# Attention scores of a chunk: three split fp32r passes in four row groups, or one fp32 pass straight from the projections

## The reference, cut to what matters

```
q = silu(to_heads(q)); k = silu(to_heads(k)); v = to_heads(v)
qkv_none_diag = einsum('bhmd,bhde->bhme', qi * q_decay, kv)
qk       = einsum('bhmd,bhsd->bhms', qi, ki) * diag_decay
qkv_diag = einsum('bhms,bhse->bhme', qk, vi)
kv_new   = block_decay * kv + einsum('bhsd,bhse->bhde', ki * k_decay, vi)
```

## Time and profile before

| | |
|---|---|
| time, 3 runs | median 572.98 us, 571.99 to 573.39 |
| profiled execution | its own time 572.29 us, span of its trace 570.6 us |
| TensorE busy | 514.4 us, 90% of the span |
| VectorE, ScalarE, GpSimd busy | 328.6, 262.3, 247.3 us |
| mean granted TensorE clock | 0.961 of full speed |

### The profile page before, as it was taken

The page is one execution under the profiler, slowest core; times in us unless marked ns, Lnnn a source line. Parts: engine busy times, 40 slices in busy tenths (PEclk is TensorE's granted clock), DMA queues, the critical chain, the costliest instruction groups (busy, mean ns, idle before and its releaser), DMA issues.

```text
span 570.6 us, 11414 instructions
## 1 busy us (share of the span) xinstructions
PE 514.4 (90%) x4523; PEld 472.3 (83%) x4523; DVE 328.6 (58%) x613; ACT 262.3 (46%) x472; POOL 247.3 (43%) x207
## 2 busy tenths in 40 slices
PE   2979999999999999999999479889989997399994
PEld 2969899998999989999898469778967876399983
DVE  5988655754387787644547855778764643012331
ACT  7822232222276668232433337656676744253340
POOL 2062454333231333343386847243433333068973
PEclk9979999999999999999999787999998998799998
DMA  8733133211311001022224315543348331424532
GB/s 258 278 96 119 47 112 112 93 57 38 112 40 36 24 20 39 20 66 69 109 93 148 116 56 174 192 166 130 118 160 277 100 138 40 147 76 152 176 115 37
DMA packets 32884, 62.11 MB, mean 109 GB/s; under 512 B 3440, under 2 KB 3456, under 8 KB 32704
## 3 DMA queue, kind: packets, MB, share of 16 engines
q1 hardware_dynamic: 32288, 60.08, 31.5%
q0 software_dynamic: 544, 1.31, 1.2%
HBM read 48.27 MB, written 13.12 MB: 108 GB/s over the span
## 4 chain that ended last, share of the span: by engine, by line
PE 58%; issue 17%; POOL 10%; DVE 8%; ACT 5%; DMA 1%; SPq 0%; DVEq 0%; POOLq 0%; ACTq 0%
PE bank L1264 19%; PE bank L1218 7%; PE bank L1219 7%; PE bank L1220 7%; PE bank L1255 6%; POOL wlo L1162 5%; PE bank L1286 3%; DVE rope L897 2%; PE bank L1332 2%; PE bank L1322 2%; PE bank L1294 2%; PE bank L1316 2%; PE bank L1234 1%; DMA UR<-uo_all 1%; DVE rope L895 1%
## 5 line engine op out<-in xcount | busy, mean ns | idle before, releaser
L1162 POOL TENSOR_TENSOR wlo<-raw,whi 128x512 fp32r<-128x512 f32 x96 | 129.9, 1386 | 122.4 <-ACT whi L521 122.4
L1218 PE MATMUL bank<-HTh,whi 128*128 128x256 f32 x224 | 66.3, 296 | 14.4 <-DVE XR L932 9.7
L1219 PE MATMUL bank<-HTl,whi 128*128 128x256 f32 x224 | 65.8, 294 | 0.0
L1220 PE MATMUL bank<-HTh,wlo 128*128 128x256 f32 x224 | 65.5, 292 | 0.0
L1143 POOL TENSOR_TENSOR state<-kv_new,state_dec 128x512 f32<-128x512 f32 x15 | 21.8, 1454 | 94.7 <-DVE kv_new L834 94.7
L823 DVE TENSOR_TENSOR A<-bank,DEC 128x512 f32<-128x512 f32 x64 | 39.7, 683 | 37.2 <-PE bank L1286 35.7
L1218 PEld LDWEIGHTS bank<-HTh,whi 128*128 128x128 f32 x224 | 45.5, 203 | 15.4 <-issue 15.1
L521 ACT ACTIVATE whi<-raw 128x2048 fp32r<-128x2048 f32 x24 | 45.8, 1910 | 16.5 <-DMA raw<-in_w_down 12.5
L1219 PEld LDWEIGHTS bank<-HTl,whi 128*128 128x128 f32 x224 | 45.5, 203 | 0.2
L1220 PEld LDWEIGHTS bank<-HTh,wlo 128*128 128x128 f32 x224 | 45.4, 203 | 0.0
L1264 PE MATMUL bank<-xTh,WKh 128*128 128x256 f32 x128 | 38.6, 302 | 2.1 <-DVE WKl L764 2.1
(11 more groups left out here) (281 smaller groups left out, 1539.4 us busy)
## 6 DMA issues: line engine op xcount, KB each, us to landing
X<-in_x SPq DMA_DIRECT2D x16, 256.0 KB, 2.9
xn_all<-XN SPq DMA_DIRECT2D x16, 256.0 KB, 2.0
uo_all<-uo SPq DMA_DIRECT2D x16, 256.0 KB, 2.6
raw<-in_wq SPq DMA_DIRECT2D x4, 1024.0 KB, 5.3
UR<-uo_all SPq DMA_DIRECT2D x16, 256.0 KB, 5.6
XR<-in_x SPq DMA_DIRECT2D x16, 256.0 KB, 4.7
raw<-in_wo SPq DMA_DIRECT2D x4, 1024.0 KB, 5.6
out<-XR SPq DMA_DIRECT2D x16, 256.0 KB, 2.9
```

The source lines that it names most:

```text
L1162: ins = Q.tensor_tensor(low[:, k, :], raw[b % 2][:, k, :], high[:, k, :].bitcast(f32), ALU.subtract)
L1218: T.matmul(dst, lh, rh, start=first, stop=False)
L1219: T.matmul(dst, lh, rl, start=False, stop=False)
L1220: return T.matmul(dst, ll, rh, start=False, stop=last)
```

## The change

`score` multiplies chunk N of KT and QT as they stand, as 16 fp32 matmuls (one for each head) instead of 48 fp32r ones. kh, kl, qh and ql, the four steps that write them and their semaphores are gone. `score` waits for the projections alone; the evacuation of new K and Q projections (`evacuate`) waits for the scores that read the old ones.

```diff
-        kh, kl, qh, ql = (at(n, 112 + 2 * i, [P, NK, P], f32r) for i, n in enumerate(("kh", "kl", "qh", "ql")))
...
                     if name == "K":
-                        act.wait_ge(q_w_lo if g else k_w_lo, NK), act.wait_ge(k_lo, used)
-                        act.wait_ge(kt_ps, used), act.wait_ge(k_hi, used)
+                        act.wait_ge(q_w_lo if g else k_w_lo, NK), act.wait_ge(s_ps, used), act.wait_ge(kt_ps, used)
                     if name == "Q":
-                        act.wait_ge(q_w_lo, NK), act.wait_ge(q_lo, used), act.wait_ge(q_dec, used)
-                        act.wait_ge(q_hi, used)
+                        act.wait_ge(q_w_lo, NK), act.wait_ge(s_ps, used), act.wait_ge(q_dec, used)
...
-            def k_high(N):
-                act.wait_ge(proj_sb, NPROJ * (N // CH) + 2)
-                act.wait_ge(s_ps, N), act.wait_ge(k_lo, N)
-                S.activation(kh[:], chunk(KT, N), ACT.Copy).then_inc(k_hi, 1)
-
-            def q_high(N):
-
-                act.wait_ge(proj_sb, NPROJ * (N // CH) + 4)
-                act.wait_ge(s_ps, N), act.wait_ge(q_lo, N)
-                S.activation(qh[:], chunk(QT, N), ACT.Copy).then_inc(q_hi, 1)
...
-            def q_low(N):
-                dve.wait_ge(q_hi, N + 1), dve.wait_ge(s_ps, N)
-                V.tensor_tensor(ql[:], chunk(QT, N), qh[:].bitcast(f32), ALU.subtract).then_inc(q_lo, 1)
...
-            def k_low(N):
-                pool.wait_ge(k_hi, N + 1)
-                Q.tensor_tensor(kl[:], chunk(KT, N), kh[:].bitcast(f32), ALU.subtract).then_inc(k_lo, 1)
...
             def score(N):
 
-                pe.wait_ge(k_hi, N + 1), pe.wait_ge(q_hi, N + 1)
-                pe.wait_ge(k_lo, N + 1), pe.wait_ge(q_lo, N + 1)
-                pe.wait_ge(masked, 4 * N)
+                pe.wait_ge(proj_sb, NPROJ * (N // CH) + 4), pe.wait_ge(masked, 4 * N)
...
                 for j in range(NK):
-                    for n, (k, q) in enumerate(((kh, qh), (kh, ql), (kl, qh))):
-                        for r in range(4):
-                            rows = slice(DH * r, DH * r + DH)
-                            ins = T.matmul(score_banks[r][:, j * P:(j + 1) * P], k[rows, j, :], q[rows, j, :],
-                                           start=n == 0, stop=n == 2)
+                    for r in range(4):
+                        rows = slice(DH * r, DH * r + DH)
+                        ins = T.matmul(score_banks[r][:, j * P:(j + 1) * P], chunk(KT, N)[rows, j, :],
+                                       chunk(QT, N)[rows, j, :], start=True, stop=True)
                 ins.then_inc(s_ps, 1)
```

More of the change, by code:

```diff
@@ L268, in build @@
         xt_ps, xt_hi, xt_lo, proj_ps, proj_sb = sems("xt_ps xt_hi xt_lo proj_ps proj_sb")
-        k_hi, q_hi, k_lo, q_lo, q_dec, kt_ps, k_dec = sems("k_hi q_hi k_lo q_lo q_dec kt_ps k_dec")
+        q_dec, kt_ps, k_dec = sems("q_dec kt_ps k_dec")
         s_ps, masked, inter_ps, kv_ps, kv_masked, pv_ps = sems("s_ps masked inter_ps kv_ps kv_masked pv_ps")
@@ L592, in _ @@
                 in_position(N, 0, tiles)
-                if N == -1:
-                    k_high(0)
-                    q_high(0)
                 if N >= 1:
                     mean_square(N - 1)
-                if 0 <= N < N_TILES - 1:
-                    k_high(N + 1)
-                    q_high(N + 1)
                 count_marks(ranked(N, 0))
@@ L970, in _ @@
                     key_decayed(N)
-                if -1 <= N < N_TILES - 1:
-                    q_low(N + 1)
                 in_position(N, 0)
@@ L1173, in _ @@
                     q_decayed(N)
-                if -1 <= N < N_TILES - 1:
-                    k_low(N + 1)
                 if N == HIDDEN:
```

## The result

The changed kernel takes **565.84 us** (median of 4 runs, 564.69 to 566.58), against 573.18 us for the kernel before (median of 4 runs, 571.99 to 576.35; three of them are those of the table of the time before). The medians are 7.3 us apart. The recorded ratio is 0.9853, 95% interval 0.9816 to 0.9889, so the change is faster by 6.4 to 10.5 us. The forecast was 564.5. The profiled execution took 566.07 us (span 564.3), 6.2 us less than the profiled one of before.

The account below looks back on a forecast made before the run. TensorE was taken to bound chunks 0 to 14, with a chain of waits in slot 14. Savings of 6.7 us on scores and 1.8 us in slot 14 sum to 8.5: 572.98 - 8.5 = 564.5 us, range 562 to 579.

Parts of the forecast that it names:

- The sets: Scores on TensorE: an fp32 set in row groups costs a weight load, 0.112 us; 8 sets a chunk instead of 12.
- The rival by the Trainium skill: Scores on TensorE: an fp32 matmul's two records hold each other up; 1.94 us a chunk, 578.2 us; chance 0.12.
- One matmul at a time: Scores on TensorE: fp32 matmuls in row groups don't run side by side; 3.73 us a chunk, 606.6 us; chance 0.07.
- the bound of 0.54 us a chunk: Scores on TensorE: upper bound of the saving, if a set costs only 0.10 us.
- the other 0.15 us is the entry and the exit: A chunk's scores on TensorE: 0.15 us besides the sets, kept unchanged, so 1.49 us becomes 1.04.
- 15 x 0.45: Chunks 0 to 14 on TensorE: each saves 0.45 us where TensorE never waits, 6.7 us together.
- Slot 14: Chain of 300 to 325 us: 1.1 us without ql, 0.6 to 0.7 from a faster rotation; together 1.8 us.
- the rotation gets shorter: VectorE in slot 14: the rotation, 1.77 us beside kl, loses 0.6 to 0.7 us without kl.
- The chain behind it: After slot 14: all moves by 1.8 us; TensorE's wait before unit 4 shrinks to about 0.5, block 3's stays about 6.2.
- Behind 325.57 I take the rest as rigid: After unit 5's start at 325.57 us: no instruction changes, so what follows is taken as rigid.

Follow-up runs that it names:

- e4: Kernel before with the third fp32r pass (kl by qh) of the scores left out, all four split steps kept; 568.15 us.
- e3: Changed kernel with the two loops of score exchanged, all four column tiles of one row group before the next group; 591.59 us.
- e7: Kernel before with the change for chunk 15 alone: its scores in fp32, its four splits dropped; 570.83 us against 572.34.
- e1: Kernel before with fp32 scores and the added waits in evacuate, but kh, qh, ql and kl still computed and unread; 565.14 us.
- e2: Changed kernel with one subtraction of ql's shape put back on VectorE, in slot 14 alone, without kl on GpSimd; 566.66 us.
- a0: The changed kernel run a second time, with no edit; 565.78 us.
- e5: Changed kernel with weight block 3 split earlier: high part ahead of chunk 14's square, low part ahead of chunk 14's state; 562.94 us.
- e9: The kernel of e1 run again on another chip, with no edit; 566.06 us.

## Why the prediction was right, and where not

**The sets: right, and the rival fell.** The forecast hung on one step, that an fp32 set in row groups costs a weight load, 0.112 us, as the fp32r sets do. It does from the second set on, in every chunk, and e4 shows that eight sets cost nearly the same in either type. The rival by the Trainium skill, "TensorE: Matmul & The Clock Gate", section "The mechanism", went by a list item there that lets a load overlap matmuls in flight only if the row group differs; it would have made 1.94 us a chunk and 578.2 us. The loads of one row group start every 0.112 us and so do its fp32 streams of 0.106; one after the other they would need 0.21. The trace disagrees with that item, and the measurement decides. The paragraph ahead of it in the same section has a second condition that the rival left out, a load into the background weight buffer, which is also pulled ahead; no run here shows that buffer. One matmul at a time (606.6 us) fell too. What it feared exists in another order: e3 pays 2.75 us a chunk.

One of the bounds was a misreading. The prediction took 0.81 / 8 = 0.10 us a record from the earlier trace rows. The first two of those records start 0.03 us apart, and from the second on they follow at 0.112 us, so the bound of 0.54 us a chunk had nothing under it.

**The chunk's saving: 0.38, not 0.45.** The step that failed is "the other 0.15 us is the entry and the exit", carried over unchanged. With fp32 the entry is 0.05 to 0.06 us longer (e4). Over 14 chunks the miss is 14 x 0.45 - 5.37 = 0.9 us.

**"15 x 0.45": one chunk too many.** Chunk 14's scores lie before the waits, but their saving went into one: TensorE could have come to unit 1 6.2 us earlier, but block 1's low part came only 5.77 earlier (295.40 to 289.63), and the wait for it grew from 0.29 to 0.69. The prediction counted waits from 312 us on and left out the first, 0.29 us long, which already made TensorE a follower at 300 us. Cost: its 0.45 us.

**Slot 14: right size, wrong shares.** The prediction gave 1.8 us, 1.1 for ql and 0.6 to 0.7 for a rotation that is no longer slowed by kl. Measured 1.68 in the change and 1.72 in e7. The shares came out the other way round, 0.6 for ql and 1.1 for kl (e1, e2, a0). The step that failed is that the rotation gets shorter: it stayed at 1.74, since qdec slows it now, as qdec slowed ql before (1.33 in e7, where it starts later beside qdec). What falls away is a whole turn of GpSimd's queue. Two rows could have told it: the rotation's end, 302.13 + 1.77 = 303.90, stands just behind kl's, 301.60 + 1.76 = 303.36.

**The chain behind it: right.** The wait before unit 4 was to shrink to about 0.5 us (0.62) and that for block 3 to stay at 6.2 (6.17). It also named what would be late next, the state of chunk 14 between the two blocks; e5 takes that away and gains 2.8 us.

**"Behind 325.57 I take the rest as rigid": right for the change by luck, wrong as a step.** Between 300 and 350 us the change has 17.1 us at the low clock, the same as before it, so the shift of 7.45 reached SM as 7.50. e1 has 13.7, with which 1.7 us of delay vanished, and e7 10.2, with which a gain of 1.7 grew to 2.9. So the removal of the splits, with which the kernel before is 1.3 to 1.5 us faster for chunk 15 alone (e7), shows as nothing on top of the fp32 scores (e1 565.14 and e9 566.06 against a0 565.78). By which amount the clock pays back can't be forecast from the earlier trace rows; that it can is the caveat the sum lacked.

**The account.** Forecast 8.5; less 0.9 for the entry, 0.45 for chunk 14 and 0.1 for slot 14 leaves 7.05, and that is what the trace has at unit 5 (7.45 less 0.40 of an earlier start). The medians say 7.3 (the interval of the ratio makes it 6.4 to 10.5) and, with a0, 6.7. That they meet the account is in part luck: e1, which lacks the 1.7 us of slot 14, is 7.35 us faster than the kernel before as well. What is shown as a gain of time is the cheaper scores; what the removed steps give is shown up to unit 5 and not at the end. That the last stage took 1.0 back in one profiled execution remains open; e1 and e9 scatter by 3 us there.

## What to carry to other kernels

Small matmuls with 128 weight columns were priced by their weight loads here, so count records and not arithmetic: two fp32 records beat three fp32r ones, as long as the row groups take turns matmul by matmul. Before a VectorE step is called the cost of a chain, look at what GpSimd runs beside it, and suspect an instruction that ends just behind GpSimd's of being held by it. Where the clock changes level within a stretch, a gain of a microsecond or two ahead of it is not yet a gain.

## What the runs showed of the hardware

- A weight load of 0.107 us and the stream before it overlap within one row group, in fp32r (a stream of 0.056 us, estimated from e4) and in fp32 (0.106) alike: sets at 0.112 us.
- TensorE takes records for its row groups in program order and lets only a few of one group wait: with 2 in a turn a chunk's scores last 0.90 us from the first set to the last, with 4 it is 1.02, with 8 it is 2.55.
- A 128x512 fp32 tensor_tensor of VectorE takes 0.68 us alone; started beside one of GpSimd with SBUF inputs it ends 0.54 to 0.56 us after that one, and takes 1.1 to 1.77 us.
- The change and e1's kernel, 1.7 us apart at unit 5, had their low clock between 300 and 350 us in two and in three pieces (17.1 and 13.7 us), each in two executions. Counted from chunk 14's score they reached SM within 0.2 us of each other.
